# When GpSimd sends its indirect DMAs: more marked scatters in the first sort, marks in the second layer's lead, later gathers in the first and fourth layers

## The reference

```python
edge_index = jnp.stack([src, dst])
x = x + _L0_gnn_ref(_layernorm(x, axis=-1), edge_index, L0_gnn_W, L0_gnn_a)
x = x + _L0_ffn_ref(_layernorm(x, axis=-1)[None], ...)[0]
x = x + _L1_gnn_ref(_layernorm(x, axis=-1), edge_attr_8, edge_attr_4, ..., edge_index)
x = x + _L1_ffn_ref(_layernorm(x, axis=-1)[None], ...)[0]
x = x + _L2_gnn_ref(_layernorm(x, axis=-1), src, dst, ...)
x = x + _L2_ffn_ref(_layernorm(x, axis=-1)[None], ...)[0]
x = x + _L3_gnn_ref(_layernorm(x, axis=-1), L3_gnn_W, L3_gnn_att, src, dst)
x = x + _L3_ffn_ref(_layernorm(x, axis=-1)[None], ...)[0]
```

```python
h = jax.nn.silu(edge_attr @ fc_w1 * (1.0 / np.sqrt(float(NUM_BASIS))))
h = jax.nn.silu(h @ fc_w2 * (1.0 / np.sqrt(64.0)))
w = h @ fc_w3 * (1.0 / np.sqrt(64.0))
wA, wB, wC, wD = jnp.split(w, 4, axis=1)
...
ns = jax.ops.segment_sum(mid_s, src, num_segments=N)
```

## Times and profile before

| | us |
|---|---|
| median of three runs | 5254.73 (5247.79 to 5256.63) |
| the profiled execution | 5255.74 |
| its span | 5254.0 |

### The profile page before, as it was taken

The page is one execution under the profiler, slowest core; times in us unless marked ns, Lnnn a source line. Parts: engine busy times, 40 slices in busy tenths (PEclk is TensorE's granted clock), DMA queues, the critical chain, the costliest instruction groups (busy, mean ns, idle before and its releaser), DMA issues.

```text
span 5254.0 us, 74251 instructions
## 1 busy us (share of the span) xinstructions
PE 3842.1 (73%) x19152; PEld 2547.1 (48%) x19152; DVE 3228.2 (61%) x8314; ACT 2680.5 (51%) x8902; POOL 2558.2 (49%) x2689
## 2 busy tenths in 40 slices
PE   6868888626189999869666666678999946666665
PEld 2346666525044444458444445445655534444554
DVE  9955666543359899775667777753333435555753
ACT  6835777512068888744345656553233325555522
POOL 4666555656757687316155555521000056666244
PEclk9978899858589999989778888889999967777777
DMA  3023333334133333322455555520000033333334
GB/s 123 22 71 85 82 82 82 58 70 121 27 89 90 84 91 90 48 86 81 135 150 146 148 149 151 147 72 0 7 13 15 8 94 89 90 89 88 36 119 134
DMA packets 278821, 441.37 MB, mean 84 GB/s; under 512 B 114083, under 2 KB 192782, under 8 KB 278158
## 3 DMA queue, kind: packets, MB, share of 16 engines
q0 software_dynamic: 124624, 331.70, 24.7%
q1 hardware_dynamic: 147230, 98.37, 6.6%
q10 hardware_dynamic: 6560, 6.55, 0.4%
HBM read 368.84 MB, written 67.60 MB: 83 GB/s over the span
## 4 chain that ended last, share of the span: by engine, by line
PE 52%; DVE 18%; another core or an unknown queue 11%; issue 10%; ACT 5%; DMA 2%; DVEq 2%; POOL 1%; SPq 0%; ACTq 0%; POOLq 0%
PE PB L3178 7%; PE PB L2020 7%; PE PB L2554 5%; PE PB L726 5%; PE PB L1081 4%; PE PB L3162 3%; PE PB L1576 2%; ACT XNT L2638 2%; PE PB L2030 2%; PE PB L1564 2%; PE PB L1090 2%; PE PB L2042 1%; PE PB L2037 1%; DVE bigt L705 1%
## 5 line engine op out<-in xcount | busy, mean ns | idle before, releaser
L2554 PE MATMUL PB<-XNT 128*128 128x260 f32 x1760 | 617.7, 489 | 144.5 <-DVE bigt L2526 101.3
L1022 POOL DMA_INDIRECT bigt<-HTAB,bigt x440 | 421.1, 957 | 291.5 <-ACT bigt L1111 151.9
L2672 POOL DMA_INDIRECT bigt<-ZTAB,DO x440 | 454.7, 1033 | 220.8 <-issue 112.8
L1992 POOL DMA_INDIRECT bigt<-YTAB,bigt x440 | 472.2, 1073 | 177.5 <-issue 128.5
L359 POOL DMA_INDIRECT RECS<-bigt x391 | 389.8, 997 | 228.3 <-issue 94.4
L2554 PEld LDWEIGHTS PB<-XNT 128*128 128x128 f32 x1760 | 380.0, 238 | 217.4 <-issue 104.3
L717 ACT ACTIVATE bigt<-bigt 128x128 f16<-128x128 f16 x1214 | 383.3, 389 | 149.1 <-DVE bigt L690 62.5
L2638 ACT ACTIVATE XNT<-bigt 128x65 f32<-128x65 f32 x1768 | 446.2, 336 | 0.0
L2020 PE MATMUL PB<-bigt 128*128 128x512 f32 x880 | 407.9, 606 | 7.1 <-DVE bigt L2181 4.1
L726 PE MATMUL PB<-bigt 128*128 128x440 f16 x1564 | 366.9, 359 | 52.6 <-issue 30.4
L2672 POOL DMA_INDIRECT bigt<-KVTAB,DO x296 | 282.8, 955 | 243.5 <-DVE XNT L2434 157.6
(11 more groups left out here) (490 smaller groups left out, 9540.4 us busy)
## 6 DMA issues: line engine op xcount, KB each, us to landing
bigt<-YTAB,bigt POOLq DMA_INDIRECT x552
bigt<-SRT SPq DMA_DIRECT2D x56, 128.0 KB
OUTS<-bigt SPq DMA_DIRECT2D x56, 128.0 KB
SRT<-bigt SPq DMA_DIRECT2D x11, 640.0 KB, 9.9
bigt<-HTAB,bigt POOLq DMA_INDIRECT x440
bigt<-ZTAB,DO POOLq DMA_INDIRECT x440
KVTAB<-bigt SPq DMA_DIRECT2D x25, 258.0 KB
YTAB<-bigt SPq DMA_DIRECT2D x10, 640.0 KB, 10.1
```

Of the source, the lines that this page charges most:

```text
L1022: e.indirect_dma_start(out=Gt[:, g % GB, j, :], out_offset=None, in_=HTAB, in_offset=bass.IndirectOffsetOnAxis(ap=SO[:, g * G + j:g * G + ...
L1992: e.indirect_dma_start(out=Gt[:, g % GB, j, :], out_offset=None, in_=YTAB, in_offset=bass.IndirectOffsetOnAxis(ap=SO[:, g * G + j:g * G + ...
L2554: m = e.matmul(self.PV[n % len(self.PV)], self.OH[:, g % self.MB, j, :], self.msg[:, g % self.MB, j, :], start=(k == 0), stop=(k == self.H ...
L2672: e.indirect_dma_start(out=dst[:, j, :], out_offset=None, in_=table, in_offset=bass.IndirectOffsetOnAxis(ap=DO[:, g * G + j:g * G + j + 1] ...
```

## The change

```diff
@@ the first sort, pool_sort @@
-                for c in range(150):
-                    e.wait_ge(*sort_s.rows_made.at(min(EC - 1, 13 * c // 5)))
+                for c in range(185):
+                    e.wait_ge(*sort_s.rows_made.at(min(EC - 1, 21 * c // 10)))
                     attr_scatters(e, 1)
@@ the first edge loop, pool_edges @@
                         if g >= GB and j % 2 == 0:
-                            e.wait_ge(*half(weighed, 2 * (g - GB) + j // 2))
+                            e.wait_ge(*half(added, 2 * (g - GB + 1) + j // 2))
@@ the second graph layer, pool @@
             def pool(e):
+                attr_scatters(e, 18)
+                for t in range(NT):
+                    e.wait_ge(*turns.xnt.at(t))
+                    attr_scatters(e, 1)
                 attr_scatters(e, EC)
                 e.wait_ge(*y_kept.last)
@@ the fourth graph layer, pool @@
                     if n >= 2 * GB:
-                        e.wait_ge(*att.added.at(n - 2 * GB))
+                        e.wait_ge(*att.added.at(n - 2 * GB + 3))
```

## The result

| | us |
|---|---|
| before, median of 8 runs | 5250.29 (5245.12 to 5256.63) |
| changed, median of 8 runs | 5272.91 (5264.98 to 5289.41) |
| ratio | 1.0046 (95%: 1.0031 to 1.0060) |
| changed, profiled execution / span | 5267.48 / 5265.7 |

A forecast was written before the change was run, and what follows sets the result against it. No engine was taken to bound the whole; stages were read singly, with indirect DMAs delaying marks. Lead -52, sort +26, first gate 0 and fourth gate -1 summed to -27, giving 5228 us, range 5190 to 5275.

The forecast's parts named there:

- The lead, -52: Second layer's lead: fewer, marked scatters let tiles pace at 1.45 us, first gather near 1423.5 instead of 1475.62; -52 us.
- The price of 1.40 us for each indirect DMA: Second layer's lead: 103 indirect DMAs each leave service that other engines' marks queue behind, 1.40 us for one.
- The support from the expert layer's lead: First expert layer's lead: one scatter a tile, 1.45 us a tile, read as the same price from another side.
- The sort, +26: First sort's loop: 185 scatters at 1.40 us settle at 260 us instead of 234; +26 us.
- The upper bound: First sort: 185 scatters at the first edge loop's 1.60 us each take 296 us; +62 us.
- Rival 1: Sort pays the upper bound, late marks idling VectorE; +10, or +25 with a bad edge loop: 5265 to 5280; chance 0.14.
- The first gate, 0: First layer's edge loop: later gather gate shifts waits but total service stays; 0 us, with -25 to +25.
- At the start it helps: Head of first edge loop: GpSimd's pause starts 5.5 us earlier, where VectorE's logit had waited 17.43 us.
- 440 x 1.40 = 616 us: First layer's edge loop: total service of its 440 gathers, set against 651 us, the same either way.
- rival 3: Sort hides all its scatters, +3, with -52 in the lead and -10 in the edge loops: 5196; chance 0.16.
- Rival 4: Later gathers starve an edge loop, each of 102 groups losing 0.5 us: +50, net +23, 5278; chance 0.14.
- The fourth gate, -1: Fourth layer's gathers: gate three halves later moves the train by a phase; -1 us, with -20 to +20.

The follow-up runs named there:

- k3_rows32: Kernel before, but each of the 78 scatters in the second layer's lead writes 32 of its 128 rows; 5323.2 us, ratio 1.0021, slow series.
- e4_lead_marks: Kernel before with only marks in the second layer's lead: 53 scatters at once, 25 behind one tile each; 4723.7 us, ratio 1.0000, quick series.
- the last series: Fifth series, slow, kernel before 5267.0 us: whole change ratio 1.0032, first layer's gate alone 1.0024, marks in the lead alone 0.9991.
- the fourth: Fourth series, slow, kernel before 5329.6 us: first layer's gate alone 1.0000, sort's part alone 1.0002, 28 lead scatters moved to the expert loop 1.0015.
- the quick series: First two series, kernel before 4724 us: parts alone, whole change (0.9905), and 28 lead scatters moved to the expert loop (1.0002).

## Why the prediction was wrong

**The lead, -52: right.** -51.8 in the first comparison, -50.5 in the last. The tiles of the changed kernel stand 1.56 us apart (37.5 us for 25, 36 forecast), the first gather 23 us behind the last tile (21.2). The price of 1.40 us for each indirect DMA was confirmed by five counts of them and, with fewer rows, by k3_rows32 (1.405). What I put down to the marks is the number of scatters: marks alone gave 4 us of lead. The support from the expert layer's lead, 1.45 us a tile, was weaker than it looked: without late marks its tiles already stand 1.13 us apart (e4_lead_marks), and those of the second layer 0.66.

**The sort, +26: mis-sized, it was +48.4.** The step that failed is "The scatters wait for VectorE in turn, so it settles where both agree: 185 x 1.40 = 260 us". The loop does not settle at a full load of 1.40 but at 1.53 to 1.56 us a scatter, as 165, 185 and 190 of them show. My reading: a mark that queues behind a few DMAs makes VectorE idle, and in that time no new row lets a scatter go. The 44 us of idle time on VectorE bear it out, but how much of the size is the waits themselves and how much TensorE's lower clock (0.88 for 0.99, up to 13 us) stays open. The upper bound, 1.60 from the edge loop, was the nearer row. Rival 1 named the mechanism; that the whole came out within its 5265 to 5280 is partly luck, since its sort was to cost 62 us and the gate made up the rest.

**The first gate, 0: wrong in the first comparison and in the last series, right in the fourth.** To the last addition the loop took 20.7 us more in the first comparison, 13 more when the gate was alone in the last series, and no more in the fourth. The sentence that failed to see a cost is "At the start it helps". I counted the stall of VectorE that ends 5 us earlier, and it does, but not the gathers that GpSimd no longer sends meanwhile: it stands 14 us at the head of the stream. In the last series that loss was not made up, in the fourth it was, so the pause alone does not explain the loss. Why the old gate's loop takes 729 to 777 us in the slow traces, and the new gate's 750 to 769, stays open. The load was also misread: 440 x 1.40 = 616 us belong to the 704.7 us of all gathers, not to 651. In the quick series the sort hid its scatters as in rival 3 (+2 us); the rest of that rival did not come (lead -44 for -52, edge loops unchanged for -10). Rival 4 (gathers too late for their use) was not seen: the longer waits are of GpSimd for additions and of VectorE for marks.

**The fourth gate, -1:** 672.6 to 677.4 us, and 674.5 to 681.4 in the last series, of which 1 and 4 come back in the stretch behind. What is left, 3 to 4 us, is within what these loops differ by from run to run (with the old gate 673.6 to 676.5 us in the last series, 681.1 to 688.1 in the fourth), and alone in a slow series it was not tried.

**The sum.** -52 was matched by +48, and what is left is the first gate's: in the last series the gate alone costs 13 us of the 17 that the whole costs there.

No kernel tried was faster than before in a slow series. In a quick one the sort's part alone and the whole change are equal, 0.9911 and 0.9905.

## What to carry to other kernels

Work that is moved under another loop is free only while that loop can pass it without waiting. Where the work waits for the loop's marks and delays them too, take the rate from a loaded loop of the same kernel (here 1.60 us, and 1.53 to 1.56 were measured), not from a train that waits for nothing (1.40). For a gate that is moved later, look at the pause at the head of the stream as well as at the stall that it shortens, and measure such a loop to its last use and not to its last gather: here that changed 20 us of loss into 13, and 3 to 5 us into none. And run the kernel before beside the change: the same edit was worth -44 us where before took 4724 us and +17 where it took 5267.

## What the runs showed of the hardware

The kernel before took 4724 us in two series and 5250 to 5330 us in the others, with the same instructions and durations: ScalarE's copy 0.38 to 0.39 us, a scatter's issue 0.97 us, a packet of GpSimd's DMAs 0.17 us in the mean, in both. What differs is how soon a semaphore mark arrives while GpSimd issues indirect DMAs: 0.03 us or some 4.4. In the slow case each indirect DMA takes 1.40 us of something that marks queue behind, for 128 rows as for 32, and for longer than its packets move.

The traces' own records of semaphore updates differ as well. All eight quick traces hold about 62,200 of them, all twelve slow ones 29,900 to 32,300, for the same program. In a quick lead (e4_lead_marks) each scatter leaves 16 increments, most of them 8 ns apart. In a slow one (before) one or two of the 16 are recorded for each scatter, at the pace of the issue (1398.44, 1399.72, 1400.98), and the mark that lets ScalarE start at 1404.40 is stamped 1404.38. So the delay lies ahead of the recorded update, and not between it and ScalarE. As missing records name no releaser, they may also be why these waits end in "remote" so often.

The Trainium skill, DMA: Bandwidth & Descriptors, section "Why a DMA increments its semaphore by 16 and not by 1", lets all 16 engines post an increment for each DMA that GpSimd issues, which fits a price that does not depend on rows. By it the 1.40 us would be some 0.09 us for each increment, an estimate that no run tests. Why marks are late in one series and not in another, on a chip of the same number, is open; so is whether the recording of the updates has a part in it.
